# An attention kernel on one core: a group's token transposes spread over three steps, and the centring moved from ScalarE to VectorE

## The chip, the core and the metric

The kernel runs on one core of a Trainium2 chip. The metric is the device time of one execution in microseconds (us). Instructions run on TensorE (PE in the profile; PEld is its weight load), VectorE (DVE), ScalarE (ACT), GpSimd (POOL) and SyncE (SP), which here issues all DMAs. Each engine works through its own list in order; semaphores tie the lists together.

## The reference

For 64 graphs of 128 tokens with 512 features, two masked attention passes (8 heads of 64) and a feed-forward network, with residuals and layer norms:

```python
edge_features = _attn(eq, nk, nv, n2e_mask)          # queries, keys, values from x
edge_features = _ln(edge_features + pe, norm1_g, norm1_b)
node_updates = _attn(nq, ek, ev, incidence_matrix)   # queries from x; keys, values from edge_features
node_features = _ln(pe + node_updates, norm2_g, norm2_b)
h = jax.nn.gelu(_lin(node_features, ffn_w1, ffn_b1), approximate=False)
out = _ln(node_features + _lin(h, ffn_w2, ffn_b2), norm3_g, norm3_b)
```

The result is `_layernorm(x + out)`, in fp32. The layer norm behind each attention pass is what the change touches: (x - m) / sqrt(v + eps), then gain and shift.

## The kernel before, in words

**Stages.** Attention pass 0 (16 groups of 4 graphs), attention pass 1 (16 groups more, numbered 16 to 31), then the feed-forward pass (16 groups). A product in fp32 is made as three products of a high and a low part, so every operand is split on ScalarE (high) and on VectorE or GpSimd (low).

**A group.** `body` runs once for each group on each engine, with four steps u = 0 to 3, one for each pair of heads. TensorE's step is, in order: keys (12 matmuls), queries (12), `weigh` (40 small ones, softmax times values), values (12, for a later use) and scores (12). The softmax runs a step behind: in step u ScalarE and VectorE work on the scores of step u-1. VectorE masks and takes the maximum (L763), ScalarE does the exponentials (L525) and the high parts (L532, keys L512 and L514, queries L519), VectorE the low parts (L772, L744, L747, and the queries' L752), then `add_weighed` (L684: L688, L701, L706), which scales the weighed sum, adds the tokens and takes statistics. The scores of a step wait for the queries' low part (L913).

**The norm of a group.** `weigh` of a group ends in step 1 of the next group's body; there `add_weighed` also aggregates the moments (L710). GpSimd's `inverse_spread` (L611) makes rstd, and -mean and -mean times rstd for ScalarE, and then adds the value bias to the tokens of pair 3 (`add_bias`, L651). In step 2 ScalarE centres the four graphs (`centre`, L482), behind its high part of the queries. In step 3 TensorE transposes the tokens of graph 0 ahead of the keys, of graph 1 ahead of the queries, of graph 2 behind `weigh` and of graph 3 ahead of the scores (`turn`, L833: four 128x128 transposes into one PSUM bank, `turn_bank`). ScalarE's `copy_turned` (L473) empties the bank with gain and shift into `turned`, which has two halves; `turn` b waits for copy b-1 (L836). SP stores each half to HBM (`store_turned`, L387), the input of a later pass.

**What sets the order.** It is written out by hand for each engine. `over_groups` (L104) unrolls the first two and the last two groups of a pass and loops over the twelve between, two in a turn: a jump back stands ahead of groups 4, 6, 8, 10, 12 and 20, 22, 24, 26, 28. In pass 1, ScalarE and GpSimd also split the queries' source of the next group in step 3 (L534, L636), GpSimd's part ahead of `add_bias` of pair 3. Between the passes the weights are split anew. The last group's norm and transposes run inside the first feed-forward group (L1038 to L1041).

Of the kernel before, what the change touches and what calls it, by code (L numbers as in the profile page):

```python
# [120 lines left out]
class Shared:  # L121
# [3 lines left out]
    def __init__(self, nc, ctx):  # L125
# [3 lines left out]
        def sem(n):  # L129
# [24 lines left out]
            "minus_mean": [P, GB], "offset": [P, GB], **NORM_TILES}.items()}  # L154
# [74 lines left out]
def attention_passes(nc, ctx, m, block, passes, feed_forward, nodes_features, residual, identity_in):  # L229
# [53 lines left out]
    stats, minus_mean, offset = (small[n] for n in ("stats", "minus_mean", "offset"))  # L283
# [43 lines left out]
    spread_ready, negated, rstd_ready, offset_ready = sem("spread_ready"), sem("negated"), sem("rstd_ready"), sem("offset_ready")  # L327
# [71 lines left out]
    def _(sp):  # L399
# [14 lines left out]
        def body(g, parity, before, own, after):  # L414
# [6 lines left out]
            if not below(g, 2):  # L421
                store_turned(sp, g - 2, own, GB - 1)
# [18 lines left out]
            if not starts(g):  # L441
                turn_probabilities(sp, C * g - 1)

# [5 lines left out]
            turn_probabilities(sp, C * g + 1)  # L449

# [22 lines left out]
    def copy_turned(act, g, own, b):  # L473
        act.wait_ge(turned_ready, GB * g + b + 1)
# [6 lines left out]

    def centre(act, g, parity, b):  # L482
        if b == 0:
            act.wait_ge(offset_ready, g + 1)
        data = total[parity][:, b, :]
        nc.scalar.activation(data, data, ACT.Identity, bias=offset[:, b:b + 1], scale=rstd[:, b:b + 1]).then_inc(centred, 1)

    @block.scalar
    def _(act):
# [64 lines left out]
        def body(g, parity, before, own, after):  # L554
# [8 lines left out]
            for u in range(C):  # L563
# [22 lines left out]
                if turning:  # L586
                    copy_turned(act, g - 1, before, 1)
                query_high(g, own, u)
                if u < 2:
                    split_source(g, parity, range(2 * u, 2 * u + 2))  # L590
                if u == 2 and not starts(g):
                    for b in range(GB):
                        centre(act, g - 1, 1 - parity, b)
                if turning:
                    if own == 1 and after == 1:
                        split_queries(g + 1)
                    copy_turned(act, g - 1, before, 2)
                    copy_turned(act, g - 1, before, 3)
# [12 lines left out]
    def inverse_spread(pool, g):  # L611
# [6 lines left out]
        pool.wait_ge(negated, g + 1)  # L618
        pool.wait_ge(rstd_ready, g + 1)
        nc.gpsimd.tensor_tensor(offset[:], minus_mean[:], rstd[:], ALU.mult).then_inc(offset_ready, 1)  # L620

    @block.gpsimd
    def _(pool):
# [58 lines left out]
        over_passes(pool, body)  # L682

# [29 lines left out]
    def _(dve):  # L713
# [68 lines left out]
        def body(g, parity, before, own, after):  # L782
# [8 lines left out]
            for u in range(C):  # L791
# [22 lines left out]
                query_low(g, own, u)  # L814
                if u == 2 and own != after:
# [44 lines left out]
    def _(pe):  # L860
# [15 lines left out]
        def values(g, parity, own, b):  # L876
# [4 lines left out]
            for c in range(C):  # L881
                if opens(g) and b == 0:
# [3 lines left out]
                                                                          [w[:, c, :] for w in (wh["v"], wl["v"])]), range(c, c + 1))  # L886

# [39 lines left out]
        def body(g, parity, before, own, after):  # L927
            if ends(g):
                return
            for u in range(C):  # L930
                turning = u == C - 1 and not starts(g)
# [31 lines left out]
    def centre_final(act):  # L963
# [474 lines left out]
```

## Time and profile before

| | us |
|---|---|
| median of 3 runs | 3041.64 (3040.52 to 3041.72) |
| the profiled execution, its own time | 3036.6 |
| its span, first to last instruction | 3034.8 |
| TensorE busy in it | 2895.0 |

The profiled execution lasted 1.8 us longer than its span, and 5.0 us less than the median of the runs. Attention fills the first 1570 us or so of the span. A timeline row reads: start, length, engine, line, operation, written tile <- read tiles, shapes, how many rows are merged, and in brackets how long the engine was idle before and what ended it.

### The profile page before, as it was taken

The page shows a single profiled execution, that of the slowest core. Times are in us where ns is not written, and L with a number is a line of the kernel's source. Part 1 is how long each engine was busy: PE and PEld are TensorE (multiplying, and loading weights), DVE is VectorE, ACT ScalarE, POOL GpSimd, SP SyncE. Part 2 cuts the span into 40 slices and gives each one's busy share as a digit, 9 for nine tenths or more (in the row PEclk, how much of TensorE's full clock was granted, in tenths as well). Part 3 has the DMA queues.
Part 4 walks back from the last instruction along what each step waited for, and adds up shares of the span by engine and source line. Part 5 has one row for each costly group of instructions (what it writes and reads, how often), then busy time and mean ns, then how long its engine had stood idle before and what let it go on. Part 6 is the DMA issues. An engine that isn't in the chain of part 4 may idle for free.

```text
span 3034.8 us, 55254 instructions
## 1 busy us (share of the span) xinstructions
PE 2895.0 (95%) x17920; PEld 2397.2 (79%) x17920; DVE 1618.3 (53%) x5786; ACT 1633.8 (54%) x4266; POOL 1297.0 (43%) x1291
## 2 busy tenths in 40 slices
PE   8999999999899999999989999999999999999996
PEld 7888878788787777787867888888888888888885
DVE  7776877777776767676763323232332323233234
ACT  6778777778788887888874222222222222222221
POOL 3443534344355555555431443444344344434434
PEclk9999999999999999999999999999999999999998
DMA  6554544454566565656563011111011111100101
GB/s 192 119 117 119 116 113 111 110 124 118 131 161 157 149 163 143 167 142 163 139 171 118 29 56 49 56 55 55 28 35 55 48 55 55 55 28 34 56 35 63
DMA packets 488660, 295.40 MB, mean 97 GB/s; under 512 B 279585, under 2 KB 410785, under 8 KB 488481
## 3 DMA queue, kind: packets, MB, share of 16 engines
q1 hardware_dynamic: 488480, 293.49, 36.2%
q8 instruction: 53, 0.87, 0.1%
q14 instruction: 127, 1.03, 0.1%
HBM read 159.21 MB, written 67.11 MB: 75 GB/s over the span
## 4 chain that ended last, share of the span: by engine, by line
PE 58%; issue 21%; POOL 14%; ACT 3%; DVE 2%; DMA 1%; POOLq 0%; SPq 0%; ACTq 0%; DVEq 0%
PE proj L1336 23%; PE score L1350 12%; PE proj L1350 11%; PE proj L872 9%; POOL att_tokens L651 4%; POOL att_v L633 3%; POOL source_lo L646 3%; PE score L919 2%; POOL att_v L631 2%; POOL att_query_lo L640 1%; PE att_out L856 1%; ACT att_probs L525 1%; ACT turned L478 1%; POOL pool_scratch L101 1%; POOL att_rstd L617 1%
## 5 line engine op out<-in xcount | busy, mean ns | idle before, releaser
L1122 ACT ACTIVATE hidden<-proj,ffn_bias 128x512 f32<-128x512 f32 x256 | 176.4, 689 | 1016.5 <-PE proj L1336 1016.5
L1282 DVE TENSOR_TENSOR hidden_lo<-hidden,hidden_hi 128x512 fp32r<-128x512 f32 x256 | 203.6, 795 | 966.2 <-ACT hidden_hi L1115 966.2
L525 ACT ACTIVATE att_probs<-att_probs,att_minus_max 128x128 f32<-128x128 f32 x1024 | 397.2, 395 | 115.5 <-DVE att_minus_max L763 115.5
L101 POOL TENSOR_TENSOR pool_scratch<-pool_scratch 128x1 f32<-128x1 f32 x144 | 41.4, 288 | 731.2 <-DVE ffn_moments L1226 415.2
L772 DVE TENSOR_TENSOR att_p_lo<-att_probs,att_p_hi 128x512 f16<-128x512 f32 x256 | 188.5, 776 | 292.0 <-ACT att_p_hi L532 292.0
L763 DVE CUSTOM_DVE_ANT_0 att_probs<-score,att_mask 128x128 f32<-128x128 f32 x1024 | 226.3, 285 | 29.2 <-issue 15.6
L646 POOL TENSOR_TENSOR source_lo<-source_raw,source_hi 128x512 fp32r<-128x512 f32 x128 | 163.0, 1295 | 152.0 <-ACT source_hi L548 152.0
L478 ACT ACTIVATE turned<-att_turn,att_shift,att_gain 128x128 f32<-128x128 f32 x512 | 193.2, 459 | 63.6 <-PE att_turn L838 62.2
L872 PE MATMUL proj<-weight_v_hi,source_hi 128*128 128x512 f32 x512 | 211.9, 414 | 13.6 <-DVE weight_v_lo L722 11.1
L872 PE MATMUL proj<-source_hi,weight_k_hi 128*128 128x512 f32 x512 | 203.4, 397 | 3.7 <-DVE weight_k_lo L722 3.7
L1336 PE MATMUL proj<-source_hi,w_hi 128*128 128x512 f32 x512 | 201.7, 394 | 0.0
L1336 PE MATMUL proj<-source_lo,w_hi 128*128 128x512 f32 x512 | 201.7, 394 | 0.0
L1336 PE MATMUL proj<-source_hi,w_lo 128*128 128x512 f32 x512 | 201.7, 394 | 0.0
L872 PE MATMUL proj<-weight_v_hi,source_lo 128*128 128x512 f32 x512 | 201.6, 394 | 0.0
L525 ACT ACTIVATION_READ_ACCUMULATOR att_probs<-att_probs,att_minus_max 128x1 f32 x1024 | 197.6, 193 | 6.4 <-issue 6.4
L872 PE MATMUL proj<-source_hi,weight_k_lo 128*128 128x512 f32 x512 | 201.1, 393 | 0.0
L872 PE MATMUL proj<-source_lo,weight_k_hi 128*128 128x512 f32 x512 | 200.8, 392 | 0.0
L872 PE MATMUL proj<-weight_v_lo,source_hi 128*128 128x512 f32 x512 | 200.7, 392 | 0.0
L856 PEld LDWEIGHTS att_out<-att_v,att_pt_hi 128*128 128x128 f16 x3072 | 149.1, 98 | 37.8 <-issue 37.8
L1213 POOL TENSOR_TENSOR normed<-normed,gain_row 128x512 f32<-128x512 f32 x64 | 83.9, 1311 | 211.6 <-DMA normed<-nodes 211.6
L651 POOL TENSOR_TENSOR att_tokens<-att_tokens,bias_row 128x512 f32<-128x512 f32 x128 | 167.9, 1312 | 1.7 <-DMA att_tokens<-in_x 1.7
L919 PE MATMUL score<-att_k_hi,att_q_hi 128*128 128x256 f32 x512 | 148.6, 290 | 18.9 <-DVE att_q_lo L752 18.9
(159 smaller groups left out, 8550.3 us busy)
## 6 DMA issues: line engine op xcount, KB each, us to landing
att_tokens<-in_x SPq DMA_DIRECT2D x128, 256.0 KB, 3.0
source_raw<-in_x_t SPq DMA_DIRECT2D x16, 1024.0 KB, 5.7
edges_t<-turned SPq DMA_DIRECT2D x64, 256.0 KB, 2.5
source_raw<-edges_t SPq DMA_DIRECT2D x16, 1024.0 KB, 5.8
att_query_raw<-in_x_t SPq DMA_DIRECT2D x16, 1024.0 KB, 6.6
nodes_t<-turned SPq DMA_DIRECT2D x64, 256.0 KB, 2.6
source_raw<-nodes_t SPq DMA_DIRECT2D x16, 1024.0 KB, 7.9
normed<-nodes SPq DMA_DIRECT2D x16, 1024.0 KB, 5.7
```

The source lines that it names most:

```text
L478: last = nc.scalar.activation(turned[:, b % 2, c, :], turn_bank[:, c * P:(c + 1) * P], ACT.Identity, bias=shift_column[own][:, c:c + 1], s ...
L525: nc.scalar.activation(probs[:, j, :], probs[:, j, :], ACT.Exp, bias=minus_max[:, j:j + 1], scale=-1.0, accum_out=row_sum[:, side, j:j + 1 ...
L646: nc.gpsimd.tensor_tensor(source_lo[1 - parity][:, c, :], source_raw[:, c, :], source_hi[1 - parity][:, c, :].bitcast(F32), ALU.subtract). ...
L651: nc.gpsimd.tensor_tensor(pair(tokens, u), pair(tokens, u), bias_v[:, u * P:(u + 1) * P].rearrange("p (o d) -> p o d", o=1).to_broadcast([ ...
L763: nc.vector.tensor_tensor_reduce(out=probs[:, 4 * h + j, :], in0=score_bank[h][:, j * P:(j + 1) * P], in1=mask[:, 2 * h + j // 2, :], scal ...
L772: nc.vector.tensor_tensor(p_lo[:, 4 * h:4 * h + 4, :], probs[:, 4 * h:4 * h + 4, :], p_hi[:, 4 * h:4 * h + 4, :], ALU.subtract).then_inc(p ...
L856: last = nc.tensor.matmul(out, p, value, start=(i == 0), stop=(i == len(products) - 1))
L872: last = nc.tensor.matmul(bank[:], stationary, moving, start=(c == 0 and i == 0), stop=(c == C - 1 and i == 2))
L919: last = nc.tensor.matmul(score_bank[h][:, 2 * i * P:2 * (i + 1) * P].rearrange("p (s j) -> p s j", s=2), q, k, start=(n == 0), stop=(n == 2))
L1282: nc.vector.tensor_tensor(hidden_lo[:, c % 2, :], hidden[:, c % 2, :], hidden_hi[:, c % 2, :].bitcast(F32), ALU.subtract).then_inc(hidden_ ...
L1336: last = nc.tensor.matmul(up_bank[c % 2][:], w, s, start=(i == 0), stop=(i == len(products) - 1))
L1350: last = nc.tensor.matmul(down_bank[b][:], h, w, start=(c == 0 and i == 0), stop=(c == FC - 1 and i == 2))
```

## The change

On TensorE the transposes of a group go to other places: graph 0 in step 2 behind `weigh`, graph 1 in the middle of step 2's values (after two of four chunks), graph 2 in step 3 behind `weigh`, and graph 3 in step 0 of the body after, behind `weigh`. ScalarE's copies follow them: copies 0 and 1 at the end of step 2, copy 2 in step 3, copy 3 in step 0 after the split of the source. The stores on SP move: store 0 behind the softmax transposes of step 2, store 3 behind the first ones of the next body. The centring goes to VectorE: four `tensor_scalar` (subtract the mean, multiply by rstd) in step 2, behind the queries' low part and ahead of `add_weighed` and, at the change of passes, of the split of the value weights. GpSimd no longer makes -mean and offset. The last group's centring in the feed-forward pass goes to VectorE's step 4 from ScalarE's step 5. Group 30, which has no values behind it in step 2 and 3, has transposes 1 and 3 ahead of the scores.

```diff
@@ SP, body of a group
             load_tokens(sp, g, own, 1)
-            if not below(g, 2):
-                store_turned(sp, g - 2, own, GB - 1)
...
             if not starts(g):
                 turn_probabilities(sp, C * g - 1)
+            if not below(g, 2):
+                store_turned(sp, g - 2, own, 3)
...
             turn_probabilities(sp, C * g + 1)
+            if not starts(g):
+                store_turned(sp, g - 1, before, 0)
...
             if not starts(g):
-                store_turned(sp, g - 1, before, 0)
                 store_turned(sp, g - 1, before, 1)
@@ ScalarE, body of a group
-                turning = u == C - 1 and not starts(g)
-                if turning:
-                    copy_turned(act, g - 1, before, 0)
...
                 key_high(g, own, u)
-                if turning:
-                    copy_turned(act, g - 1, before, 1)
                 query_high(g, own, u)
                 if u < 2:
                     split_source(g, parity, range(2 * u, 2 * u + 2))
+                if u == 0 and not below(g, 2):
+                    copy_turned(act, g - 2, own, 3)
                 if u == 2 and not starts(g):
-                    for b in range(GB):
-                        centre(act, g - 1, 1 - parity, b)
-                if turning:
+                    copy_turned(act, g - 1, before, 0)
+                    copy_turned(act, g - 1, before, 1)
+                if u == 3:
                     if own == 1 and after == 1:
                         split_queries(g + 1)
-                    copy_turned(act, g - 1, before, 2)
-                    copy_turned(act, g - 1, before, 3)
+                    if not starts(g):
+                        copy_turned(act, g - 1, before, 2)
+                    if at(g, last_group - 1):
+                        copy_turned(act, g - 1, before, 3)
@@ GpSimd, inverse_spread
-        nc.gpsimd.tensor_scalar(minus_mean[:], moments[:, :, 0], -1.0, None, ALU.mult).then_inc(negated, 1)
...
-        nc.gpsimd.tensor_tensor(offset[:], minus_mean[:], rstd[:], ALU.mult).then_inc(offset_ready, 1)
@@ VectorE
+    def centre(dve, g, parity):
+        dve.wait_ge(rstd_ready, g + 1)
+        for b in range(GB):
+            data = total[parity][:, b, :]
+            nc.vector.tensor_scalar(data, data, moments[:, b, 0:1], rstd[:, b:b + 1], ALU.subtract, ALU.mult).then_inc(centred, 1)
...
                 query_low(g, own, u)
+                if u == 2 and not starts(g):
+                    centre(dve, g - 1, 1 - parity)
@@ TensorE, values: for each chunk c
+                if midway is not None and c == 1:
+                    turn(pe, *midway)
@@ TensorE, body of a group
-                if turning:
-                    turn(pe, g - 1, 1 - parity, 0)
                 keys(g, parity, own, u)
-                if turning:
-                    turn(pe, g - 1, 1 - parity, 1)
                 queries(g, parity, own, u)
                 if u >= 2:
                     weigh(pe, g, parity, u - 2)
+                    if u == 2 and not starts(g):
+                        turn(pe, g - 1, 1 - parity, 0)
                 elif not starts(g):
                     weigh(pe, g - 1, 1 - parity, u + 2)
-                if turning:
+                if u == 0 and not below(g, 2):
+                    turn(pe, g - 2, parity, 3)
+                if u == 3 and not starts(g):
                     turn(pe, g - 1, 1 - parity, 2)
                 if u < 2:
                     values(g, parity, own, u + 2)
                 elif not at(g, last_group - 1):
-                    values(g + 1, 1 - parity, after, u - 2)
-                if turning:
-                    turn(pe, g - 1, 1 - parity, 3)
+                    values(g + 1, 1 - parity, after, u - 2, (g - 1, 1 - parity, 1) if u == 2 and not starts(g) else None)
...
                 scores(g, u, 0)
                 scores(g, u, 1)
```

## Rows read from the trace of the kernel before

**Rows 1.** Page, part 1: busy us (share of the span) xinstructions of each engine.
```profile
PE 2895.0 (95%) x17920; PEld 2397.2 (79%) x17920; DVE 1618.3 (53%) x5786; ACT 1633.8 (54%) x4266; POOL 1297.0 (43%) x1291
```

**Rows 2.** Waits of PE: us in total, times, longest.
```profile
PE att_turn L838 <- ACT turned L478: 62.2, 47, 3.4
PE score L919 <- DVE att_q_lo L752: 18.9, 12, 2.6
```

**Rows 3.** Timeline, PE, plain group, first pass: start, length, engine, line, operation, [idle before].
```profile
663.14 0.48 PE L872 MATMUL proj<-weight_v_hi,source_hi 128*128 128x512 f32 x1
...
665.99 0.28 PE L919 MATMUL score<-att_k_hi,att_q_hi 128*128 128x256 f32 x1
...
676.72 0.63 PE L838 MATMUL att_turn<-att_identity,att_even_sum 128*128 128x128 f32 x4 [1.57 <-ACT turned L478]
...
677.11 0.48 PE L872 MATMUL proj<-weight_v_hi,source_hi 128*128 128x512 f32 x1
...
680.32 0.36 PE L919 MATMUL score<-att_k_hi,att_q_hi 128*128 128x256 f32 x1
```

**Rows 4.** Timeline, DVE, step two of the same group.
```profile
663.38 0.75 DVE L752 SCALAR_TENSOR_TENSOR att_q_lo<-proj,att_bias_q,att_q_hi 128x512 fp32r<-128x512 f32 x1
664.05 0.19 DVE L688 RECIPROCAL att_row_inverse<-att_row_sum 128x8 f32<-128x8 f32 x1
...
666.91 0.29 DVE L763 CUSTOM_DVE_ANT_0 att_probs<-score,att_mask 128x128 f32<-128x128 f32 x1
```

**Rows 5.** Timeline, POOL, step two of the same group.
```profile
662.28 1.04 POOL L617 TENSOR_TENSOR att_rstd<-att_spread,minus_half 128x4 f32<-128x4 f32 x1
...
663.61 1.29 POOL L651 TENSOR_TENSOR att_tokens<-att_tokens,bias_row 128x512 f32<-128x512 f32 x1
```

**Rows 6.** Timeline, DVE, feed-forward pass: two centrings of four instructions.
```profile
1836.75 1.91 DVE L1231 TENSOR_SCALAR normed<-normed,ffn_moments,ffn_rstd 128x512 f32<-128x512 f32 x4
...
1892.01 3.87 DVE L1231 TENSOR_SCALAR normed<-normed,ffn_moments,ffn_rstd 128x512 f32<-128x512 f32 x4
```

**Rows 7.** Timeline, PE, last group of the attention: third and fourth transposes.
```profile
1565.97 0.63 PE L838 MATMUL att_turn<-att_identity,att_even_sum 128*128 128x128 f32 x4 [3.45 <-ACT turned L478]
...
1568.29 1.09 PE L838 MATMUL att_turn<-att_identity,att_even_sum 128*128 128x128 f32 x4 [1.69 <-ACT turned L478]
```

**Rows 8.** Timeline, PE, group behind a loop edge, first pass.
```profile
583.91 0.36 PE L919 MATMUL score<-att_k_hi,att_q_hi 128*128 128x256 f32 x1
...
596.40 0.39 PE L919 MATMUL score<-att_k_hi,att_q_hi 128*128 128x256 f32 x1 [1.31 <-DVE att_q_lo L752]
...
615.95 0.47 PE L872 MATMUL proj<-weight_v_hi,source_hi 128*128 128x512 f32 x1
...
633.10 0.36 PE L919 MATMUL score<-att_k_hi,att_q_hi 128*128 128x256 f32 x1
```

**Rows 9.** Timeline, DVE: the same group, then the change of passes.
```profile
587.53 0.06 DVE L92 MEMSET att_dve_scratch<- 128x1 f32 x1 [3.32 <-issue]
...
617.16 0.75 DVE L752 SCALAR_TENSOR_TENSOR att_q_lo<-proj,att_bias_q,att_q_hi 128x512 fp32r<-128x512 f32 x1
...
780.03 2.50 DVE L722 TENSOR_TENSOR weight_k_lo<-att_weight_k_raw,weight_k_hi 128x512 fp32r<-128x512 f32 x4 [2.51 <-ACT weight_k_hi L497]
```

**Rows 10.** Timeline, PE, second pass: a plain group, then one behind an edge.
```profile
929.72 0.36 PE L919 MATMUL score<-att_k_hi,att_q_hi 128*128 128x256 f32 x1
...
977.51 0.63 PE L838 MATMUL att_turn<-att_identity,att_even_sum 128*128 128x128 f32 x4 [0.69 <-ACT turned L478]
...
977.89 0.36 PE L919 MATMUL score<-att_k_hi,att_q_hi 128*128 128x256 f32 x1
...
1029.30 0.36 PE L919 MATMUL score<-att_k_hi,att_q_hi 128*128 128x256 f32 x1
```

**Rows 11.** Timeline, POOL, second pass, step three.
```profile
1025.88 5.03 POOL L640 TENSOR_TENSOR att_query_lo<-att_query_raw,att_query_hi 128x512 fp32r<-128x512 f32 x4 [13.08 <-ACT att_query_hi L541]
```

**Rows 12.** Windows: length, busy us of PE, PEld, DVE, ACT, POOL, granted clock, DMA share, GB/s.
```profile
1568.00:1577.00 9.00, 7.64 (x26) 6.55 (x27) 5.08 (x27) 6.08 (x23) 0.00 (x0) 0.50 1.02 278
```

More of the change, by code:

```diff
@@ L153, in __init__ @@
             "minus_max": [P, UNIT], "row_sum": [P, 2, UNIT], "row_inverse": [P, 2, UNIT], "stats": [P, GB, C, 6],
-            "minus_mean": [P, GB], "offset": [P, GB], **NORM_TILES}.items()}
+            **NORM_TILES}.items()}
         self.feed_forward = {n: sb(f"ffn_{n}", shape) for n, shape in {"bias_1": [P, FC], "stats": [P, GB, 6], **NORM_TILES}.items()}
@@ L282, in attention_passes @@
     pool_scratch = m.pool_scratch
-    stats, minus_mean, offset = (small[n] for n in ("stats", "minus_mean", "offset"))
+    stats = small["stats"]
     dve_scratch, moments, spread, rstd = (small[n] for n in NORM_TILES)
@@ L326, in attention_passes @@
     biased, summed, stats_ready, moments_ready = sem("biased"), sem("summed"), sem("stats_ready"), sem("moments_ready")
-    spread_ready, negated, rstd_ready, offset_ready = sem("spread_ready"), sem("negated"), sem("rstd_ready"), sem("offset_ready")
+    spread_ready, rstd_ready = sem("spread_ready"), sem("rstd_ready")
     centred = sem("centred")
@@ L473, in copy_turned @@
     def copy_turned(act, g, own, b):
+        own = pass_of(g, own)
         act.wait_ge(turned_ready, GB * g + b + 1)
@@ L480, in copy_turned @@
         last.then_inc(turned_copied, 1)
[L482 to L486, printed above, removed]
     @block.scalar
@@ L874, in project, with values @@
                 last.then_inc(projected, 1)
-        def values(g, parity, own, b):
+        def values(g, parity, own, b, midway=None):
             if b == 0:
@@ L930, in body @@
             for u in range(C):
-                turning = u == C - 1 and not starts(g)
-                if turning:
-                    turn(pe, g - 1, 1 - parity, 0)
                 keys(g, parity, own, u)
-                if turning:
-                    turn(pe, g - 1, 1 - parity, 1)
                 queries(g, parity, own, u)
@@ L946, in body @@
                 elif not at(g, last_group - 1):
-                    values(g + 1, 1 - parity, after, u - 2)
-                if turning:
-                    turn(pe, g - 1, 1 - parity, 3)
+                    values(g + 1, 1 - parity, after, u - 2, (g - 1, 1 - parity, 1) if u == 2 and not starts(g) else None)
+                if at(g, last_group - 1):
+                    if u == 2:
+                        turn(pe, g - 1, 1 - parity, 1)
+                    if u == 3:
+                        turn(pe, g - 1, 1 - parity, 3)
                 scores(g, u, 0)
@@ L961, in store_final_tokens @@
         sp.wait_ge(tokens_out, 16 * NG)
-    def centre_final(act):
-        for b in range(GB):
-            centre(act, final, 1, b)
     return {
@@ L973, in attention_passes @@
         "add_last": lambda dve, u: add_weighed(dve, final, 1, 1, u),
-        "centre": centre_final,
+        "centre": lambda dve: centre(dve, final, 1),
         "inverse_spread": lambda pool: inverse_spread(pool, final),
@@ L1038, in feed_forward_pass @@
     WEIGH = (0, 2)
-    CENTRE = 5
+    CENTRE = 4
     TURNS = 8
@@ L1135, in body @@
                     attention["copy_turned"](act, c - TURNS)
-                if starts(g) and c == CENTRE:
-                    attention["centre"](act)
         over_groups(act, body)
@@ L1289, in body @@
                         attention["add_last"](dve, 2 + WEIGH.index(c))
+                    if c == CENTRE:
+                        attention["centre"](dve)
                     continue
```

2 lines of the change are left out of this document (removed).

## The prediction

> **What bounds the kernel now.** I read the page's busy line first: TensorE is busy 2895.0 us of 3034.8 [rows 1], and the other engines a little over half. So a change gains only where it shortens TensorE's standstills. The waits of TensorE say which: 62.2 us before transposes, for ScalarE's copies, and 18.9 us before scores, for VectorE's low part of the queries [rows 2]. The first is what the edit goes for; 2.0% is its ceiling. The timeline of a plain group of the first pass shows where it lies: the third transpose of step 3 stands still 1.57 us, while step 2 has its values begin right behind the weighing (663.14) and its scores right behind those (665.99) [rows 3]. In the second pass the fourth transpose waits 0.69 us besides [rows 10]. The groups behind a jump back (five in each pass) lose more: VectorE restarts 3.32 us late [rows 9], and the scores of step 0 wait 1.31 us in the first pass [rows 8].
>
> **The question is step 2.** Before, nothing in TensorE's step 2 hangs on the centring; its result is wanted a step later. Now the first transpose stands behind the weighing, and the centring stands on VectorE behind the queries' low part. So I put those two moments beside each other.
>
> **First transpose, plain group.** TensorE is done weighing at 663.14 [rows 3]. VectorE starts the queries' low part at 663.38 and is ready for its next instruction 0.67 later, at 664.05 [rows 4]. TensorE reaches the transpose 0.24 us before that low part even begins. The feed-forward pass has the same operation and shape: four take 1.91 us undisturbed [rows 6], 0.48 each; for the first one to its end I take 0.54, since neighbours overlap a little (estimate). With 0.1 for the signal (my estimate), the transpose can start at 664.05 + 0.54 + 0.1 = 664.69: a new wait of 1.55 us.
>
> **GpSimd beside it.** Its bias add runs 663.61 to 664.90 now [rows 5]; without offset, which stands between rstd's end at 663.32 and the add, and -mean, ahead of rstd (some 0.4 us for both, estimate), it would run from about 663.2 to 664.5, across the moment at which the centring wants to start. The feed-forward pass shows what the two do to each other: four centrings take 1.91 us alone and 3.87 where GpSimd's multiplies run with them [rows 6], 0.49 more for each. So in the first pass I let the first centring wait for the add's end: 664.5 instead of 664.05, a wait of 2.0 us. The ends: 1.55 (no disturbance), and a whole add of 1.29 us [rows 5] in front, 2.85. In the second pass GpSimd stands idle 13.08 us there, until the split of the query source [rows 11], so 1.5 us stays.
>
> The Trainium skill, SBUF — State Buffer, Who interferes with whom, says that whichever of VectorE (in such an operation) and GpSimd starts first holds the shared pair of ports for its whole instruction. By that the centring waits for the add's end, as I take it; if it started first, the add would wait and the sum would be some 6 us less.
>
> **Second transpose.** It waits for the first copy. The round trip from one transpose to the next through ScalarE is 1568.29 - 1565.97 = 2.32 us where nothing lies between [rows 7]. Half of the values lies between now: 0.39 for a transpose from standstill (676.72 to 677.11) and 1.42, half of 663.14 to 665.99 [rows 3], 1.81 together. New wait: 0.5 us, in every group of both passes.
>
> **Third and fourth.** They stand behind step 3's and step 0's weighing, with a step's keys and queries between them and the copy they wait for. No wait. The four transposes still cost their time; two of them now follow a standstill, where one costs 0.39 instead of about 0.45 with the restart of the next matmuls. I take 0.2 us off a group (estimate from rows 3).
>
> **VectorE and ScalarE behind it.** VectorE has 1.91 us more in step 2 (2.36 with the wait for the add): its next masks, at 666.91 now [rows 4], could start at 669.3. By the waits above TensorE begins the scores at 663.14 + 2.0 + 1.81 + 0.5 + 1.81 = 669.3, and the masks need the first half of them. So `add_weighed` and the masks behind the centring hold up nobody, with some 0.9 us to spare (666.91 - 665.99), and ScalarE, relieved of four instructions, is not late either. If the cover fails, the scores of step 3 wait for the low part. **SP:** store 0 waits for its copy behind the softmax transposes of step 2, store 3 behind those of step 0; what stands behind them (token loads) is wanted a step later. I put all this at nothing; if the cover fails, a late token load shows as GpSimd waiting for DMA.
>
> **Plain group.** First pass: -1.57 + 2.0 + 0.5 - 0.2 = +0.75. Second: -1.57 - 0.69 + 1.5 + 0.5 - 0.2 = -0.45.
>
> **Group behind a jump.** VectorE is late there by the restart, so the first transpose waits longer: its low part starts at 617.16, 1.21 us behind the place of the transpose at 615.95 (0.24 in the plain group) [rows 8, 9]; with 0.67 + 0.54 + 0.1 that is 2.5, and 2.95 with the add. In return the step-0 scores, which wait for VectorE anyway, hide the fourth transpose (0.45). First pass: -1.57 + 2.95 + 0.5 - 0.2 - 0.45 = +1.2. I take the 1.21 for the second pass too, where the whole such group takes 1029.30 - 977.89 = 51.4 us, against 977.89 - 929.72 = 48.2 for a plain one [rows 10]. There ScalarE loses the fourth copy at the end of the body, which ends some 1.9 us after the scores began (2.32 - 0.38); I let that give back 0.85 of the late restart. -2.26 + 2.5 + 0.5 - 0.2 - 0.45 - 0.85 = -0.75.
>
> **Change of passes and last group.** At 780.03 VectorE had stood 2.51 us for the high part of the new weights [rows 9], which ScalarE does behind the fourth copy. That copy moves away: -1.7, between 0 and -2.51. The value weights are split 1.91 later in step 2 there, which the transposes no longer in step 3 make up. In the last group the new waits in step 2 take the place of 3.45 and 1.69 us in step 3 [rows 7]: nothing.
>
> **Sum.** 9 x 0.75 + 5 x 1.2 - 9 x 0.45 - 5 x 0.75 - 1.7 = 6.75 + 6.0 - 4.05 - 3.75 - 1.7 = +3.3 us (groups 15, 16 and 31 at the change and the end are the other three of 31). The profiled execution would go from 3036.6 to 3039.9; the runs lie 5.0 us above it, so I move their median by the same: 3041.6 + 3.3 = **3045.0 us**. The 62.2 us of waiting are mostly not removed but moved to step 2.
>
> **Rivals.**
> *Waits gone (faster).* The restart behind a jump gets shorter, since ScalarE and VectorE come to it with less work left, and the score waits (18.9 us [rows 2]) go with the longer first waits: the ten groups behind a jump cost what plain ones cost. First pass: from 49.2 (633.10 - 583.91 [rows 8]) to 48.0, -1.2 instead of +1.2, five times -2.4; second: from 51.4 to 47.7, -3.7 instead of -0.75, five times -2.95. 3045 - 12 - 15 = 3018. Half of it gives 3032, the undisturbed centring alone (-0.45 x 14) 3039. For it: 3.32 us of restart is long. Against: it begins when VectorE's last instruction ends, and that moves by tenths. Chance 0.25.
> *GpSimd in front (slower).* The bias add starts just ahead of each first centring of the first pass, not 0.8 us ahead: 0.85 more, 14 times, 3057. It decides from a shift of 0.7 us between the two engines; the two removed GpSimd steps are 0.4 of it, but in the wrong direction. With a VectorE that is late in the second pass too, 3062. Chance 0.18.
> *The clock falls.* After the 3.45 and 1.69 us of standstill the granted clock was 0.50, the lower level, for 9 us [rows 12, 7]. If waits of 3 us and 0.5 us in the groups behind a jump brought that, TensorE would lose 4.5 us each time, 5 times in the first pass: 3067. The waits of 1.57 us have not: behind one, values and a transpose take 3.21 us (677.11 to 680.32), the pace of step 2 [rows 3]. Chance 0.05. The Trainium skill, TensorE: Matmul & The Clock Gate, HAM oscillation, warns of such gaps between matmul bursts; it speaks against this change, and the trace so far shows it at the end of the attention only.
> *Not as said.* If the first transpose found its centring done, only the second's wait would be new: 62.2 - 31 x 0.5 = 47 us gained, 2995. The order on VectorE excludes this nearly. Chance 0.02.
>
> **Numbers.** The forecast has 0.50, with its own range of 3036 to 3054 (an error of 0.3 us in each of 29 groups). A difference of 0.2%, 6.1 us, is about what a measurement of this kernel can tell. Of the forecast's 0.50, 0.32 lie within that, 0.11 above and 0.07 below; of the faster rival's 0.25, 0.06 within and 0.19 below; the slower two lie above. Faster 0.07 + 0.19 + 0.02 = 0.28, same 0.38, slower 0.11 + 0.18 + 0.05 = 0.34. The range reaches into both rivals: 3029 to 3060.
>
> **What would show it.** Right: the wait of transposes for copies falls from 62.2 to some 15 us, all at the second transpose in step 2, and a new line appears, transposes waiting for VectorE's centring (or for its issue), 1.5 to 3 us, 30 times, some 55 us; plain groups of 48.0 us in the first pass and 47.7 in the second; a first centring instruction of about 1 us in the first pass and 0.54 in the second. Wrong: no wait before the first transpose; VectorE waiting for nothing in step 3; scores of step 0 without waits behind the jumps; or a granted clock below full speed inside a pass.

## The result, and the profile after

The changed kernel takes **3019.24 us** (median of 4 runs, 3018.14 to 3019.83); in the same session the kernel before took 3041.08 (3039.42 to 3041.72). The ratio is 0.9929, with a 95% interval of 0.9911 to 0.9946: faster by 21.8 us, or 0.7%. I had forecast 3045.0 within 3029 to 3060, so the forecast was wrong, and on the wrong side. The profiled execution has a span of 3016.0 us, 18.8 less than the one of before, which lay 5.0 us under its own median.

The page's busy line of the changed kernel [rows 1 answer to it]:

```profile
PE 2880.7 (96%) x17920; PEld 2406.1 (80%) x17920; DVE 1720.7 (57%) x5914; ACT 1553.0 (51%) x4138; POOL 1295.2 (43%) x1227
```

TensorE does the same 17920 matmuls and is busy 14.3 us less. That is the first surprise: the change moves waits about, and should leave TensorE's busy time alone. The waits of TensorE in the changed kernel (total, times, longest) show that they were in fact only moved:

```profile
PE att_turn L837 <- DVE normed L679: 30.2, 15, 2.4
PE att_turn L837 <- DVE att_even_sum L679: 26.5, 16, 3.4
PE att_turn L837 <- ACT turned L480: 11.5, 24, 1.7
...
PE score L920 <- DVE att_q_lo L749: 11.1, 11, 1.6
```

The waits for copies fell from 62.2 to 11.5 us and those of scores from 18.9 to 11.1, and 56.7 us of waiting for the centring are new: 79.3 us now against 81.1 [rows 2]. So the gain lies elsewhere. I followed two moments through both timelines: the scores of the last attention step start at 1569.02 us before and 1574.78 after, **5.8 us later**; the feed-forward pass, from its first to its last up step, takes 1425.6 us before (1573.01 to 2998.62) and 1402.0 after (1578.11 to 2980.08), **23.6 us less**. With 5.1 us lost up to the first up step and 0.3 gained behind the last one, these are the 18.8 us between the two spans. The attention, where everything was changed, got slower. The feed-forward pass, whose instructions are the same but for the last group's centring, got faster.

Groups of feed-forward matmuls between 1620 and 2990 us, first of the kernel before (the last number but one is the mean in ns; `proj` and `score` are the PSUM banks used):

```profile
L1336 PE MATMUL proj<-source_hi,w_hi 128*128 128x512 f32 x504 | 198.6, 394 | 0.0
...
L1350 PE MATMUL proj<-w_hi,hidden_hi 128*128 128x512 f32 x374 | 146.3, 391 | 0.0
...
L1336 PE MATMUL proj<-source_hi,weight_v_hi 128*128 128x512 f32 x240 | 93.5, 390 | 0.0
...
L1350 PE MATMUL score<-weight_k_hi,hidden_hi 128*128 128x512 f32 x120 | 47.5, 396 | 0.0
```

The same groups of the changed kernel:

```profile
L1335 PE MATMUL proj<-source_hi,w_hi 128*128 128x512 f32 x512 | 199.2, 389 | 0.0
...
L1349 PE MATMUL proj<-w_hi,hidden_hi 128*128 128x512 f32 x384 | 149.4, 389 | 0.0
...
L1335 PE MATMUL proj<-source_hi,weight_v_hi 128*128 128x512 f32 x240 | 93.4, 389 | 0.0
...
L1349 PE MATMUL score<-weight_k_hi,hidden_hi 128*128 128x512 f32 x120 | 46.7, 389 | 0.0
```

Before, the mean depends on which tiles a matmul reads: 396 ns for weight_k with hidden, 394 for the late weight blocks with source, 390 for weight_v with source. After, each of these is 389. Matmuls overlap, so the starts say more. TensorE's timeline of the kernel before, the first matmul of an up step (12 matmuls), of the down step behind it, and of the next up step:

```profile
2003.19 0.39 PE L1336 MATMUL proj<-source_hi,w_hi 128*128 128x512 f32 x1
...
2005.99 0.39 PE L1350 MATMUL score<-w_hi,hidden_hi 128*128 128x512 f32 x1
...
2008.73 0.39 PE L1336 MATMUL proj<-source_hi,w_hi 128*128 128x512 f32 x1
```

And of the changed kernel:

```profile
2006.32 0.39 PE L1335 MATMUL proj<-source_hi,w_hi 128*128 128x512 f32 x1
...
2009.04 0.39 PE L1349 MATMUL score<-w_hi,hidden_hi 128*128 128x512 f32 x1
...
2011.76 0.39 PE L1335 MATMUL proj<-source_hi,w_hi 128*128 128x512 f32 x1
```

Before: 2.80 and 2.74 us, 5.54 a step; after: 2.72 and 2.72, 5.44 a step, which 247 of its 254 step distances show. TensorE stands still in neither, and the granted clock is 1.00 in both. Over 16 groups, the 16 steps of a group cost 88.5 us before (5.49 to 5.55 each) and 87.0 after: 16 x 1.45 = 23 us, the gain of the pass.

What differs for these matmuls? An up step loads a weight block into TensorE and streams the source past it; a down step loads hidden and streams a weight block. The first blocks of the two weights lie where weight_v, weight_q (up) and weight_k (down) lay; the others, w2_1 and the late ones w1_2 to w2_3, have tiles of their own. The diff deletes two tiles, `minus_mean` and `offset`, 16 bytes a partition each, rounded up to 32 by the allocation. Every tile allocated behind them moves down by 64 bytes: the parts of the queries' source, hidden and its parts, and the weight blocks w2_1 and w1_2 to w2_3. Before, they start 64 bytes past a multiple of 128; after, at a multiple of 128. The weights v, k, q and the source are allocated ahead of the two and lie at multiples of 128 in both kernels.

**The attention.** TensorE in step 2 of a plain group of the first pass, changed kernel:

```profile
676.82 0.22 PE L855 MATMUL att_out<-att_v,att_pt_lo 128*128 128x64 bf16 x2
678.34 0.66 PE L837 MATMUL att_turn<-att_identity,att_even_sum 128*128 128x128 f32 x4 [1.30 <-DVE att_even_sum L679]
...
680.77 0.63 PE L837 MATMUL att_turn<-att_identity,att_even_sum 128*128 128x128 f32 x4 [0.39 <-ACT turned L480]
```

VectorE and then GpSimd beside it:

```profile
677.01 0.75 DVE L749 SCALAR_TENSOR_TENSOR att_q_lo<-proj,att_bias_q,att_q_hi 128x512 fp32r<-128x512 f32 x1
677.68 1.97 DVE L679 TENSOR_SCALAR att_even_sum<-att_even_sum,att_moments,att_rstd 128x512 f32<-128x512 f32 x4
```

```profile
676.74 1.27 POOL L642 TENSOR_TENSOR att_tokens<-att_tokens,bias_row 128x512 f32<-128x512 f32 x1
```

The waits are where I put them, 1.30 and 0.39 us. The bias add runs from 676.74 to 678.01, across the start of the centring at 677.68, as forecast; but the centring does not wait for its end. Its four instructions take 1.97 us, and no centring of the whole attention takes more than 0.62 us, against a median of 0.54.

Step 2 of a group behind a jump back (first pass), TensorE, and the granted clock in three windows there (last but two of each row):

```profile
630.01 1.12 PE L837 MATMUL att_turn<-att_identity,normed 128*128 128x128 f32 x4 [2.37 <-DVE normed L679]
630.78 0.78 PE L871 MATMUL proj<-weight_v_hi,source_hi 128*128 128x512 f32 x1
631.36 0.63 PE L871 MATMUL proj<-weight_v_lo,source_hi 128*128 128x512 f32 x1
631.78 0.63 PE L871 MATMUL proj<-weight_v_hi,source_lo 128*128 128x512 f32 x1
```

```profile
627.00:630.00 3.00, 0.64 (x23) 0.52 (x18) 2.95 (x6) 1.18 (x2) 2.59 (x3) 0.98 0.35 58
630.00:632.00 2.00, 1.99 (x7) 1.80 (x8) 1.97 (x7) 0.74 (x3) 0.00 (x0) 0.50 0.92 179
632.00:634.00 2.00, 2.00 (x9) 1.58 (x9) 1.97 (x10) 0.77 (x3) 0.00 (x0) 0.67 0.06 17
```

Behind the wait of 2.37 us the clock is at 0.50, its lower level of 1.2 GHz, for some 3 us: the transposes take 1.12 instead of 0.66, and matmuls start 0.42 apart instead of 0.23. This happens in four of the five groups behind a jump in the first pass and in three of the five in the second. The one that is spared in the first pass takes 50.51 us; the other four take 51.63 to 51.69, 1.1 us more. Behind the 1.30 us of the plain groups the clock stays at 1.00.

### The profile page after: what moved, and what is told of

Same layout as the page of the kernel before. It is cut to its first block, busy times and chain, and to the rows that moved or that the text cites. A ratio compares the mean times of both kernels' runs of the same rounds, so it can differ in the third digit from the quotient of the medians.

```text
span 3016.0 us, 55170 instructions
## 1 busy us (share of the span) xinstructions
PE 2880.7 (96%) x17920; PEld 2406.1 (80%) x17920; DVE 1720.7 (57%) x5914; ACT 1553.0 (51%) x4138; POOL 1295.2 (43%) x1227
## 4 chain that ended last, share of the span: by engine, by line
PE 74%; DVE 11%; ACT 6%; issue 6%; DMA 1%; POOL 0%; DVEq 0%; ACTq 0%; SPq 0%; POOLq 0%
PE proj L1335 23%; PE proj L871 20%; PE proj L1349 11%; PE score L1349 11%; ACT att_probs L521 4%; PE score L920 4%; PE att_out L855 3%; PE att_turn L837 2%; DVE att_p_lo L769 2%; DVE normed L698 2%; DVE att_k_lo L744 1%; DVE att_q_lo L749 1%; DVE att_stats L703 1%; ACT turned L480 1%; ACT att_p_hi L528 1%
## 5 line engine op out<-in xcount | busy, mean ns | idle before, releaser
L769 DVE TENSOR_TENSOR att_p_lo<-att_probs,att_p_hi 128x512 f16<-128x512 f32 x256 | 226.3, 922 | 207.5 <-ACT att_p_hi L528 207.5
L871 PE MATMUL proj<-weight_v_hi,source_hi 128*128 128x512 f32 x512 | 219.3, 428 | 12.1 <-DVE weight_v_lo L719 11.1
L642 POOL TENSOR_TENSOR att_tokens<-att_tokens,bias_row 128x512 f32<-128x512 f32 x128 | 179.0, 1399 | 0.5 <-DMA att_tokens<-in_x 0.5
L631 POOL TENSOR_TENSOR att_query_lo<-att_query_raw,att_query_hi 128x512 fp32r<-128x512 f32 x60 | 75.9, 1296 | 216.3 <-ACT att_query_hi L537 216.3
```

What stands on the lines that cost most here:

```text
L642: nc.gpsimd.tensor_tensor(pair(tokens, u), pair(tokens, u), bias_v[:, u * P:(u + 1) * P].rearrange("p (o d) -> p o d", o=1).to_broadcast([ ...
L769: nc.vector.tensor_tensor(p_lo[:, 4 * h:4 * h + 4, :], probs[:, 4 * h:4 * h + 4, :], p_hi[:, 4 * h:4 * h + 4, :], ALU.subtract).then_inc(p ...
L871: last = nc.tensor.matmul(bank[:], stationary, moving, start=(c == 0 and i == 0), stop=(c == C - 1 and i == 2))
```

## The experiments

Each run is compared with runs of the kernel before on the same chip, whose median was 3038 to 3040 us there; ratios are to those.

**1. The changed kernel with the old addresses (e1_shifted).**

```diff
-            **NORM_TILES}.items()}
+            "spare": [P, 16], **NORM_TILES}.items()}
```

Expected: 

> The changed kernel with a spare tile of 64 bytes a partition where minus_mean and offset stood, so that all tiles allocated behind it lie as in the kernel before (64 bytes past a multiple of 128); no instruction differs. Theory 'addresses': the feed-forward step (one up to the next) goes back from 5.44 to about 5.53 us, 23.6 us in all, and the queries of the second pass from 389 to about 395 ns a matmul (up to 3 us): 3019.2 + 24 = 3043, between 3040 and 3047. Rival 'work moved off ScalarE and GpSimd, or the new order, makes the feed-forward faster': 3019, step 5.44.

Measured: 3045.05 us, ratio 1.0019 (1.0010 to 1.0029). The step is 5.54 us again, and the means of its groups (1620 to 2990 us) are those of before, to a nanosecond:

```profile
L1335 PE MATMUL proj<-source_hi,w_hi 128*128 128x512 f32 x496 | 195.4, 394 | 0.0
...
L1349 PE MATMUL score<-weight_k_hi,hidden_hi 128*128 128x512 f32 x122 | 48.4, 396 | 0.2 <-DVE normed L1296 0.2
```

Not an instruction differs from the changed kernel, and 25.8 us are gone. Without the addresses the change makes the kernel slower by 0.1 to 0.3%; I had forecast 0.1% for it.

**2. The kernel before with the new addresses (e2_before_aligned).**

```diff
-        self.half = sb("minus_half", [P, GB])
+        self.half = sb("minus_half", [P, 2 * GB])
-        self.pool_scratch = sb("pool_scratch", [P, 4])
+        self.pool_scratch = sb("pool_scratch", [P, 4 + GB])
...
-    stats, minus_mean, offset = (small[n] for n in ("stats", "minus_mean", "offset"))
+    stats, minus_mean, offset = small["stats"], half[:, GB:2 * GB], pool_scratch[:, 4:4 + GB]
```

Expected: 

> The kernel before with minus_mean and offset put into unused columns of two tiles that exist, so that every tile behind lies where the changed kernel has it (multiple of 128); no instruction differs but in these addresses. 'Addresses': feed-forward step 5.44 instead of 5.53 us and second-pass queries as in the changed kernel: 3041.1 - 24 = 3017, and by the attention's own difference of 5.8 us below the changed kernel: 3013, between 3011 and 3018. Rival: 3041, step 5.53.

Measured: 3013.42 us, ratio 0.9914 (0.9898 to 0.9931); the step is 5.44. The group that stands first above (1620 to 2990 us):

```profile
L1336 PE MATMUL proj<-source_hi,w_hi 128*128 128x512 f32 x512 | 199.4, 389 | 0.0
```

The old order with the new addresses is 5.8 us faster than the changed kernel (4.6 by the ratios). The two effects of the change are thereby separated from both sides: the addresses are worth 24.9 us here and 25.8 in experiment 1, the new order costs 5.8 here and 6.7 there. That the attention's end had also moved by 5.8 is partly chance, since the addresses touch the attention too: a plain group of its second pass takes 48.17 us before and 48.01 here.

**3. Hidden and the late weights shifted (e3_hidden_and_late_weights).**

```diff
+            sb("spare_0", [P, 16])
             self.hidden = sb("hidden", [P, 2, GT], F32)
```

Expected: 

> The changed kernel with 64 bytes put in ahead of the hidden tiles: hidden, its high and low part and the weight blocks w1_2 to w2_3 are shifted by 64, w2_1 and the attention's tiles are not. 'Addresses': feed-forward steps slow as before (5.50 to 5.55), nearly all of the 23.6 us: 3038 to 3043. If only the weights that are loaded into TensorE matter, the down matmuls on weight_k and w2_1 (hidden loaded) are slow too and the up matmuls on weight_v and weight_q are not. Rival: 3019.

Measured: 3043.75 us, ratio 1.0018 (1.0008 to 1.0027): nearly the whole price without touching the attention's tiles. The down matmuls on weight_k take 396 ns, the up matmuls on weight_v 390 to 391.

**4. The late weights alone (e4_late_weights_only).**

```diff
             self.hidden_lo = sb("hidden_lo", [P, 2, GT])
+            sb("spare_1", [P, 16])
```

Expected: 

> The changed kernel with 64 bytes put in behind the hidden tiles: only w1_2 to w2_3 are shifted. 'Addresses': steps 0 to 7 of a feed-forward group stay at 5.44, steps 8 to 15 are slow (at most 5.54): 8 x 16 x 0.1 = 13 us at most, 3019 to 3032; which of the two rows is slow says whether the loaded operand (up: w1_2, w1_3) or the streamed one (down: w2_2, w2_3) counts. Rival: 3019 and 5.44 everywhere.

Measured: 3038.37 us, ratio 0.9999 (0.9989 to 1.0008): 19 us, more than the 13 that I allowed. Most steps on the first weight blocks stay at 5.44, those on the shifted ones take 5.56 to 5.60, of which 2.80 (up) and 2.76 to 2.80 (down), and those at the borders lie between. Its groups:

```profile
L1336 PE MATMUL proj<-source_hi,w_hi 128*128 128x512 f32 x504 | 199.1, 395 | 0.0
...
L1350 PE MATMUL proj<-w_hi,hidden_hi 128*128 128x512 f32 x377 | 148.1, 393 | 0.0
...
L1336 PE MATMUL proj<-source_hi,weight_q_hi 128*128 128x512 f32 x248 | 96.6, 389 | 0.0
```

So a loaded operand (up) and a streamed one (down) both cost when they alone are shifted. And my bound failed on something telling: the down matmuls on late weights are slower here (2.76 to 2.80), with hidden in place, than before (2.74), where hidden was shifted as well. That suggested that the two operands count against each other.

**5. Everything shifted alike (e5_all_shifted).**

```diff
+        self.spare = sb("spare", [P, 16])
         self.weight_hi = {w: sb(f"weight_{w}_hi", [P, C, D], F32R) for w in "vkq"}
```

Expected: 

> The changed kernel with a spare 64 bytes a partition ahead of all tiles: every operand of the matmuls, weights, source and hidden alike, lies 64 bytes past a multiple of 128. In the runs so far the down step costs 2.80 us where the hidden part is shifted and weight_k is not, but 2.74 where both are. Theory 'the two operands against each other': all are shifted alike, so the feed-forward step stays near 5.44 (at most 5.48) and the time at 3019 to 3026. Theory 'each operand by its own address': the step is at 5.53 or above, in the attention's keys, queries and values too: 3043 to 3070.

Measured: 3018.37 us, ratio 0.9934 (0.9919 to 0.9949), step 5.44. One group stands for all (1620 to 2980 us):

```profile
L1336 PE MATMUL proj<-source_hi,w_hi 128*128 128x512 f32 x505 | 196.4, 389 | 0.0
```

With all operands 64 bytes off, nothing is lost. It is the offset between the loaded and the streamed operand that costs, not the address of either.

**6. Half the shift (e8_shifted_32).**

```diff
+            "spare": [P, 8], **NORM_TILES}.items()}
```

Expected: 

> As e1 with 32 bytes instead of 64: query parts, hidden and late weights lie 32 bytes past a multiple of 128. If any offset off the multiple of 128 (or of 64) costs the same: 3040 to 3047, steps of 5.50 to 5.55. If only an odd multiple of 64 costs: 3019 and 5.44.

Measured: 3044.74 us, ratio 1.0022 (1.0012 to 1.0031): 32 bytes between the operands cost as much as 64 (1620 to 2990 us):

```profile
L1335 PE MATMUL proj<-source_hi,w_hi 128*128 128x512 f32 x496 | 196.4, 396 | 0.0
```

Other offsets weren't tried, nor what in the chip is behind it.

**7. The centring alone (e7_centring_alone).** The changed kernel with transposes, copies and stores at their places of before (the core of the edit):

```diff
-                    if u == 2 and not starts(g):
-                        turn(pe, g - 1, 1 - parity, 0)
...
+                if turning:
+                    turn(pe, g - 1, 1 - parity, 0)
                 keys(g, parity, own, u)
```

Expected: 

> The changed kernel with the transposes, copies and stores back at their places of before: only the centring is on VectorE. Theory 'the loss in the attention comes from the first transpose's new place behind the centring': the waits for the copies stay at 61 us, no wait for the centring: within 3 us of the aligned kernel before, 3010 to 3017. Rival 'VectorE is short of time in step 2, its masks come up to 1.8 us late': scores wait more, 3025 to 3060.

Measured: 3015.41 us, ratio 0.9924 (0.9909 to 0.9940), 2.0 us above the aligned kernel before, and the intervals overlap. Waits for copies 66.7 us, scores 8.7. In the old places the engine of the centring matters next to nothing; VectorE was not short of time in step 2. One place stands out: the group ahead of the change of passes takes 54.75 us against 51.27. There TensorE's first values wait for the new value weights, whose split on VectorE now stands behind the centring (the profile names no releaser, only "issue"):

```profile
PE proj L867 <- issue: 5.4, 1, 5.4
```

In the aligned kernel before, the same line has 2.5 us. Of the 2.9 us more, 1.9 are the centring; another 1.1 is the softmax's low part ahead of it on VectorE, which took 2.37 us instead of 1.29; why is open. The clock is at 0.50 there for 6.8 us, against 3.4.

**8. Two transposes later, the centring left on ScalarE (e6_two_transposes_later).** The aligned kernel before, with:

```diff
-                if turning:
-                    turn(pe, g - 1, 1 - parity, 2)
+                if u == 0 and not below(g, 2):
+                    turn(pe, g - 2, parity, 3)
...
-                    values(g + 1, 1 - parity, after, u - 2)
-                if turning:
-                    turn(pe, g - 1, 1 - parity, 3)
+                    values(g + 1, 1 - parity, after, u - 2, (g - 1, 1 - parity, 2) if turning else None)
```

(`values` calls the transpose behind three of its four chunks; the last group keeps its order.) Expected: 

> The kernel before with the changed kernel's addresses (3013.4 so far) and the centring left on ScalarE; of the four transposes in step 3, the third goes from behind the weighing to behind three quarters of the values, and the fourth to step 0 of the next group behind the weighing, with its copy and store; nothing else. Theory 'the wait for the second copy was the kernel's loss, and it needs only later places, not another engine': most of the 61 us before transposes go, scores wait a little more: 3013 less 35 to 55 = 2958 to 2978. Rival 'VectorE and ScalarE set the pace of a step, so the wait comes back ahead of the scores': 3000 to 3015.

Measured: **2972.47 us**, ratio 0.9787 (0.9773 to 0.9800): 41 us below the aligned kernel before and 47 below the change (43 by the ratios). The waits of TensorE:

```profile
PE score L925 <- DVE att_q_lo L756: 27.6, 12, 2.8
...
PE att_turn L842 <- ACT turned L479: 4.7, 2, 3.0
```

In the aligned kernel before, the same lines had 61.0 and 19.2. So 56 us of waits before transposes went, and 8.4 came back ahead of the scores. A plain group takes 45.48 us in the first pass (47.17 in the aligned kernel) and 45.97 in the second (48.01). The groups behind a jump don't all share in it: in eight of the ten the clock falls to 0.50 behind score waits of 2.2 to 2.8 us, as it does in one of the ten in the aligned kernel, and the five of the first pass take 4.0 us more together.

**9. The same with the centring on VectorE (e9_later_and_centring).** Experiment 8's edit on experiment 7's kernel. Expected: 

> e6 (two transposes later, 2972.5) with the centring on VectorE as in the change. Theory 'the centring's engine is worth next to nothing': within 4 us of e6, 2969 to 2977. Rival 'with ScalarE 2 us freer in step 2 the 27.6 us of score waits that e6 has left go too': 2945 to 2966. Rival 'VectorE, 2 us fuller in step 2, is late with the masks, which nothing on TensorE covers any more': 2980 to 3010.

Measured: 2988.74 us, ratio 0.9836 (0.9822 to 0.9849), 16 us above experiment 8, where I had expected 4 at most. The third reading named its size. By the end of the attention 14.8 us are lost: 3.5 in the group ahead of the change of passes (the line of experiment 7 has 5.4 us here, 2.5 in experiment 8), 2.3 in the last group, the rest in tenths in plain groups and up to 2.0 in those behind jumps. The two groups behind jumps that lose most, 1.4 and 2.0, are those in which the clock falls to 0.50 here and not in experiment 8. Score waits grew only from 27.6 to 31.3; whether late masks are the cause of the rest wasn't settled.

**10. The change with the first transpose at half the values (e10_first_at_half).**

```diff
-                    if u == 2 and not starts(g):
+                    if u == 2 and at(g, last_group - 1):
                         turn(pe, g - 1, 1 - parity, 0)
...
-                    values(g + 1, 1 - parity, after, u - 2, (g - 1, 1 - parity, 1) if u == 2 and not starts(g) else None)
-                if at(g, last_group - 1):
-                    if u == 2:
-                        turn(pe, g - 1, 1 - parity, 1)
+                    values(g + 1, 1 - parity, after, u - 2, (g - 1, 1 - parity, 0) if u == 2 and not starts(g) else None)
+                if u == 2 and not starts(g):
+                    turn(pe, g - 1, 1 - parity, 1)
```

(On ScalarE the second copy moves behind the values' high part.) Expected: 

> The changed kernel with the first transpose of step 2 not right behind the weighing but behind half of the values, and the second ahead of the scores; their copies follow (the second's behind the values' high part). Theory 'the change lost by the place, since the centring ends only 1.0 to 2.4 us behind the weighing, and in the groups behind a jump the clock falls with that wait': 1.42 us of cover for the first transpose: its waits go from 56.7 to under 20 us, the second's stay near 11, no half clock in the loops: 3019 less 38 to 50 = 2969 to 2981. Rival 'VectorE, fuller by 1.9 us in step 2, sets the pace, so the wait comes back ahead of the scores or in the next softmax': 2995 to 3019.

Measured: 2975.50 us, ratio 0.9785 (0.9768 to 0.9801), 44 us below the change. The waits, and the two windows behind the first transpose of the group that was shown at half clock (it starts at 612.84 here, after a wait of 0.91):

```profile
PE att_turn L838 <- ACT turned L480: 14.2, 31, 1.7
PE score L921 <- DVE att_q_lo L750: 11.9, 11, 1.8
...
PE att_turn L838 <- DVE normed L680: 8.6, 10, 0.9
...
PE att_turn L838 <- DVE att_even_sum L680: 4.3, 7, 3.2
```

```profile
612.80:614.80 2.00, 1.96 (x10) 1.44 (x10) 1.96 (x7) 1.18 (x4) 0.00 (x0) 1.00 0.90 178
614.80:616.80 2.00, 1.61 (x14) 1.56 (x14) 1.97 (x12) 1.67 (x5) 0.00 (x0) 1.00 0.27 79
```

The wait for the centring falls from 56.7 to 12.9 us. Among the ten groups behind a jump the clock falls in one instead of seven; those of the first pass take 49.2 to 49.6 us instead of 50.5 to 51.7. The centring may stand on VectorE; it was the first transpose that stood 1.4 us too early. (The second moved as well, and its waits are about what they were, 14.2 us.) Experiments 8 and 10 are within each other's intervals, and both beat both kernels.

## Why the prediction was wrong

**The step that failed** is the part on GpSimd: "without offset ... and -mean ... (some 0.4 us for both, estimate)". I priced the two deleted instructions and not the two deleted tiles. Their addresses carry 23 to 26 us, some seven times my whole sum. What ruled it out stands in the prediction's first paragraph: "So a change gains only where it shortens TensorE's standstills". The gain came where TensorE never stands still. By the trace of before it could have been asked: the same matmul shape took 390, 391, 394 and 396 ns there, depending on the tiles alone. I read the attention and took the feed-forward pass for settled.

**The sum of what I did price** was +3.3 us; at equal addresses it is +5.8 (experiment 2 to the change, 4.6 by the ratios) or +6.7 (before to experiment 1). With the old addresses the change takes 3045.05, beside a forecast of 3045.0; on that chip the kernel before was 2.75 us faster than in the first session, so the agreement is good to a few us and no better.

Point by point, measured as the distance from one group's last scores to the next's, against [rows 3, 8, 10]:

| | forecast | measured |
|---|---|---|
| nine plain groups, first pass | 9 x 0.75 = +6.75 | +0.7 |
| five behind a jump, first pass | 5 x 1.2 = +6.0 | +12.0 |
| nine plain groups, second pass | 9 x -0.45 = -4.05 | -6.1 |
| five behind a jump, second pass | 5 x -0.75 = -3.75 | -3.1 |
| change of passes (groups 15, 16) | -1.7 | +0.6 |
| last group | 0 | +1.0 |

With 0.7 more ahead of the first of these groups the right column gives +5.8. It holds the addresses too: at equal ones the nine plain groups of the second pass come to -4.7 (experiment 2 to the change) or -5.6 (before to experiment 1), and the whole to +4.6 or +9.2 in these single traces. In the first pass the error on the plain groups, -6.0, and that on the groups behind a jump, +6.0, cancel, so the nearness of the sums is partly luck.

*First transpose, first pass:* I took 2.0, with the bias add in front; it was 0.96 to 1.30 in most plain groups. By my undisturbed end of 1.55 the plain groups would have come to +0.28 each. My 0.1 for the signal had no row behind it; from the first centring's end (677.68 + 0.60) to the transpose at 678.34 it was 0.06. The Trainium skill, SBUF — State Buffer, Who interferes with whom, on which I leaned there, has the second engine fully blocked where VectorE works in one of its 2-port modes, a condition that I passed over; no run here shows the mode. Here the centring began within the bias add and lost at most 0.07 us, and the measurement decides.

*First transpose, second pass:* 1.47 to 1.65 in most plain groups, as forecast (1.5). *Second transpose:* 0.39 a time and 11.5 in all, against 0.5 and 15.

*Groups behind a jump:* the wait of 2.37 was less than my 2.95, but the clock came on top. I had that as a rival at 4.5 us a time with a chance of 0.05; it came seven times in the groups behind jumps, at 1.1 us in the first pass, since the low level lasted 3 us, not 9, and once more at the change of passes. The Trainium skill, TensorE: Matmul & The Clock Gate, HAM oscillation, warned of such gaps, and the 0.50 behind 2.37 us of standstill agrees in kind. I wrote that the trace of before shows it at the end of the attention only. That was misread: it is also at the start of the second pass, behind one wait, and lasts some 3.4 us there (TensorE, then the window, before):

```profile
782.58 0.79 PE L872 MATMUL proj<-source_hi,weight_k_hi 128*128 128x512 f32 x1 [3.69 <-DVE weight_k_lo L722]
...
782.00:786.00 4.00, 3.42 (x9) 2.73 (x10) 3.26 (x6) 2.60 (x6) 0.00 (x0) 0.57 0.00 0
```

*Change of passes:* the 2.51 us of [rows 9] are gone, as forecast; the next line is VectorE's same instruction in the changed kernel:

```profile
794.27 2.50 DVE L719 TENSOR_TENSOR weight_k_lo<-att_weight_k_raw,weight_k_hi 128x512 fp32r<-128x512 f32 x4 [0.17 <-ACT weight_k_hi L493]
```

But the group ahead of it became longer by 2.3 us. There TensorE waits 3.44 us for the centring, and the clock falls for 6 us, as these windows of the changed kernel show:

```profile
774.00:777.00 3.00, 1.34 (x5) 0.97 (x6) 3.00 (x7) 1.08 (x4) 0.00 (x0) 0.50 0.46 89
777.00:780.00 3.00, 3.00 (x9) 2.31 (x10) 2.96 (x12) 0.42 (x2) 0.00 (x0) 0.50 0.43 113
```

I had let the step without transposes make up for the later centring and split there; it did not. The 2.3 us are not all the change's: experiment 2, in the order of before, takes 51.27 us for this group, 1.5 more than before, and there the clock fell behind a wait of 2.53 us that before has as well, without such a fall.

**The rivals.** "Waits gone" named 3018, and 3019 was measured, but its mechanism did not happen: groups behind a jump got longer in the first pass. "GpSimd in front" fell: the adds start ahead of the centring and do it no harm. "The clock falls" was half right.

## What to carry to other kernels

When a stage that nobody edited changes its pace, compare the addresses: deleting or adding a small tile shifts every tile allocated behind it. Keep the loaded and the streamed operands of hot matmuls at the same offset from a multiple of 128 bytes (0, 32 and 64 bytes were tried here, in fp32 alone). And where an instruction waits for work that ends a known time later, move it behind that much other work of its own engine: 1.4 us of values ahead of a group's first transpose, with the second moved behind the rest of them, gave 44 us here.

## What was not expected of the hardware

Twelve fp32 matmuls of 128x512 start 2.72 us apart from the next twelve in kernels where the operands of the feed-forward pass all lie alike modulo 128 bytes, all at 0 or all at 64, and up to 2.80 where one operand is 32 or 64 bytes off the other: 227 against 233 ns a matmul, without a wait or a clock change that the profile shows. Steps next to such ones pay a little too, although their own operands lie alike: in the kernel before, down steps on w2_1 and the late blocks (both operands at 64) take 2.74 to 2.76 us and up steps on weight_v and weight_q (both at 0) 2.73 to 2.75, and within the latter the first six matmuls start up to 233 ns apart and the last six 227.

The Trainium skill, SBUF — State Buffer, Operand start alignment, treats the start address as a matter of what is allowed and says that its runs timed nothing; Who interferes with whom gives TensorE two independent read ports. What the runs show is that TensorE's pace depends on how its two operands lie to each other; whether that arises at the ports was not tried.

A standstill of 2.3 us brought the lower clock level for some 3 us in seven of the ten groups behind a jump of the changed kernel, and one of 1.3 us never did. The length of the standstill alone doesn't settle it: 2.34 us left the clock at 1.00 in one of these groups, while 1.95 to 2.02 us brought the fall in three groups of experiment 7 and 1.81 in one of experiment 10.
